# Transposing DMA transfers in place of TensorE transposes for the normalised tokens of a window-attention block

## The reference

```
f = x.transpose(0, 2, 3, 1)
f = _ln(f, g1, b1)                                   # layer norm over the 96 channels
f = jnp.roll(f, (-SS, -SS), axis=(1, 2))
win = _window_partition(f)                           # 49 tokens a window
qkv = win @ w_qkv + b_qkv
attn = jnp.einsum('bhid,bhjd->bhij', q, k) * scale   # + mask, softmax
out = jnp.einsum('bhij,bhjd->bihd', attn, v).reshape(-1, L, C)
out = out @ w_proj + b_proj                          # back to the image, rolled back
f = residual + f.transpose(0, 3, 1, 2)
m = _ln(f.transpose(0, 2, 3, 1), g2, b2)
m = jax.nn.gelu(m @ w_fc1 + b_fc1, approximate=False) @ w_fc2 + b_fc2
return f + m.transpose(0, 3, 1, 2)
```

## Time and profile before

| | |
|---|---|
| time, median of 3 runs | 2865.55 us (2864.36 to 2867.81) |
| span of the profiled execution, first to last instruction | 2865.7 us |
| PE, DVE, ACT, POOL busy | 2765.1 (96%), 2349.2 (82%), 2136.4 (75%), 1810.7 (63%) us |
| DMA engines busy, mean of 16 | 46.8% on SP's queue |

### The profile page before, as it was taken

How to read it: one execution, slowest core, us unless ns; L and a number is a source line. 1 busy time by engine, 2 the same in 40 slices (tenths; PEclk the granted TensorE clock), 3 DMA queues, 4 the chain that set the end, 5 groups by cost and what they waited for, 6 DMA issues and landing times.

```text
span 2865.7 us, 137800 instructions
## 1 busy us (share of the span) xinstructions
PE 2765.1 (96%) x55491; PEld 2312.9 (81%) x55491; DVE 2349.2 (82%) x6634; ACT 2136.4 (75%) x3464; POOL 1810.7 (63%) x2344
## 2 busy tenths in 40 slices
PE   4899999999999999999999999999999999999997
PEld 2788888888888888888888888888888888888885
DVE  7788888888888888888888888888888888888885
ACT  2677777777777777777777777777777777777774
POOL 3566666656666666666665665666666666666565
PEclk7999999999999999999999999999999999999998
DMA  2544545444554544454455455454455445454441
GB/s 72 135 125 129 132 124 132 128 130 127 131 133 125 132 131 126 129 132 124 127 132 131 125 133 133 125 132 131 126 132 132 124 129 129 129 132 128 131 117 35
DMA packets 414850, 358.86 MB, mean 125 GB/s; under 512 B 63646, under 2 KB 414176, under 8 KB 414204
## 3 DMA queue, kind: packets, MB, share of 16 engines
q1 hardware_dynamic: 414220, 350.04, 46.8%
HBM read 193.29 MB, written 154.14 MB: 121 GB/s over the span
## 4 chain that ended last, share of the span: by engine, by line
PE 91%; ACT 4%; issue 2%; DVE 2%; POOL 1%; SPq 0%; DMA 0%; POOLq 0%; DVEq 0%
PE psum L529 19%; PE psum L511 11%; PE psum L652 9%; PE psum L437 9%; PE psum L493 8%; PE psum L569 7%; PE psum L554 6%; PE psum L617 6%; PE psum L447 6%; ACT probs L713 4%; PE psum L607 3%; PE psum L455 3%; PE psum L472 2%; PE psum L596 1%; DVE nmax L849 0%
## 5 line engine op out<-in xcount | busy, mean ns | idle before, releaser
L713 ACT ACTIVATE probs<-psum 113x784 f32<-113x784 f32 x768 | 633.2, 824 | 358.9 <-PE psum L511 341.4
L849 DVE TENSOR_REDUCE nmax<-psum 113x16 f32<-113x784 f32 x768 | 745.1, 970 | 97.1 <-PE psum L493 97.0
L529 PE MATMUL psum<-vbd,probs 128*49 128x18 f32 x24576 | 642.4, 197 | 7.6 <-issue 7.0
L398 POOL TENSOR_SCALAR ve<-mv 112x7 f32<-112x7 f32 (+1 forms) x264 | 65.9, 250 | 915.0 <-PE psum L569 672.8
L529 PEld LDWEIGHTS psum<-vbd,probs 128*49 128x49 f32 x24576 | 632.2, 126 | 10.7 <-issue 10.5
L511 PE MATMUL psum<-qbd,kst 128*49 128x196 f16 x6144 | 404.7, 250 | 34.4 <-DVE xfl L884 5.7
L493 PE MATMUL psum<-kbd,qst 128*49 128x196 f16 x6144 | 404.5, 250 | 5.3 <-DVE nmax L849 3.4
L405 POOL TENSOR_TENSOR rs<-ve,half 112x7 f32<-112x7 f32 (+1 forms) x264 | 394.7, 1495 | 0.0
L410 POOL TENSOR_TENSOR xn<-xn,rs 112x672 f32<-112x672 f32 (+1 forms) x264 | 342.6, 1298 | 73.9 <-POOL rs L405 73.9
L884 DVE TENSOR_TENSOR xfl<-psum,xfh 96x784 f16<-96x784 f32 (+1 forms) x264 | 252.9, 958 | 160.7 <-ACT xfh L725 159.6
L873 DVE BATCH_NORM_STATS2 st<-tok 112x6 f32<-112x96 f32 x1824 | 318.1, 246 | 59.0 <-ACT tok L720 45.0
(11 more groups left out here) (96 smaller groups left out, 6129.4 us busy)
## 6 DMA issues: line engine op xcount, KB each, us to landing
stack_pages<-nat SPq DMA_DIRECT2D x256, 294.0 KB, 3.0
kst<-stack_pages SPq DMA_DIRECT2D x256, 220.5 KB
qbd<-stack_pages SPq DMA_DIRECT2D x1024, 55.1 KB
stack_pages<-nat SPq DMA_DIRECT2D x256, 147.0 KB, 2.0
xr<-in_x_dram SPq DMA_DIRECT2D x224, 147.0 KB, 2.7
out_dram<-yr SPq DMA_DIRECT2D x224, 147.0 KB, 2.3
qst<-stack_pages SPq DMA_DIRECT2D x256, 73.5 KB
kbd<-stack_pages SPq DMA_DIRECT2D x1024, 18.4 KB
```

The source lines that it names most:

```text
L529: last = nc.tensor.matmul(dst[:, :, h, :], probs[:, b.c % 2, h // 4, p, h % 4 * L:(h % 4 + 1) * L], vbd[:, b.c % 4, p * NH + h, :, :], sta ...
L713: nc.scalar.activation(probs[0:PR, b.c % 2, u, :, :].rearrange("j (g q) k -> j g (q k)", g=2), wide_bank()[0:PR, LEFT:LEFT + 8 * SPAN].rea ...
L849: nc.vector.tensor_reduce(dst, psum[0:PR, A:A + 2, 0:2 * CH].rearrange("i g (q h j) -> i g q h j", q=2, j=L), axis=AX.X, op=ALU.max, negat ...
```

## The change

The transposes of `back`, the ACT copy `back_high` and the DVE subtraction `back_low` are removed. POOL now makes the two float16 parts while the tokens are still on partitions (`xn16`, padded from 96 to 128 columns, with a column of ones for the biases), and SP issues two transposing transfers for each step, one for each part, that write `xfs` with channels on partitions. DVE takes over two small operations (the negated mean `less`, the variance with epsilon `ve`); POOL's two wide operations become one `tensor_scalar` for each group of 112 tokens, with two operands by partition. FC1 of both bands goes through `A`, the second after the GELU of the first, and PE's order is changed around it.

```
-            def back(t):
-                for at, g in enumerate(order + order[-1:] if odd(t) and has(t.step(HIDDEN[0])) else order):
-                    last = nc.tensor.transpose(wide_bank()[0:C, LEFT + at * SPAN:LEFT + (at + 1) * SPAN], xn[:, b.c % 2, g, :], ident[0:SPAN, 0:SPAN])
...
-                nc.scalar.activation(parts_of(xfh, b), by_channel(b), ACT.Copy).then_inc(n_high, 1)
...
-                nc.vector.tensor_tensor(parts_of(xfl, b), by_channel(b), parts_of(xfh, b), ALU.subtract).then_inc(n_low, 1)
...
+            def by_channel(b):
+                n, groups = b.c % 2, spans(b)
+                wait(sp, v_made, min(b.c - 3, NB))
+                alone(sp)
+                wait(sp, fc1_made, b.count(1, -11))
+                alone(sp)
+                for part, ready in ((HIGH, n_high), (LOW, n_low)):
+                    sp.wait_ge(ready, b.count(1, 1))
+                    alone(sp)
+                    sp.dma_start_transpose(xfs[:, b.c % 4, part, :, :].rearrange("c k t -> c (k t)")[:, 0:groups * SPAN].rearrange("c (g t) -> c g t", t=SPAN),
+                                           xn16[:, n, part, 0:groups, :].rearrange("t g c -> t (g c)")).then_inc(n_in[b.c % 4], 16)
...
             def normalise(b):
+                pool.wait_ge(stats_shared, b.count(1, 1))
+                nc.gpsimd.tensor_tensor(rs[:, n, 0:groups], ve[:, n, 0:groups], half[0:SPAN, 0:groups], ALU.pow).then_inc(root_done, 1)
+                pool.wait_ge(root_done, b.count(1, 1))
+                for g in range(groups):
+                    last = nc.gpsimd.tensor_scalar(xn[:, n, g, :], tok[:, n, g, :], less[:, n, g:g + 1], rs[:, n, g:g + 1], ALU.add, ALU.mult)
+                last.then_inc(normed, 1)
+                wait(pool, n_in[b.step(-2).c % 4], b.step(-2).used(4, N_IN))
+                nc.gpsimd.tensor_copy(xn16[:, n, HIGH, 0:groups, 0:C], xn[:, n, 0:groups, :]).then_inc(n_high, 1)
+                pool.wait_ge(n_high, b.count(1, 1))
+                nc.gpsimd.tensor_tensor(xn16[:, n, LOW, 0:groups, 0:C], xn[:, n, 0:groups, :], xn16[:, n, HIGH, 0:groups, 0:C], ALU.subtract).then_inc(n_low, 1)
...
             def expand(t, n):
                 if n == 0:
+                    for ahead in (b.step(AFTER), b.step(1 + AFTER)):
+                        pe.wait_ge(n_in[ahead.c % 4], ahead.used(4, N_IN))
+                    if has(t.step(SCORE)):
+                        pe.wait_ge(s_maxed, t.step(SCORE).count(QUADS, QUADS))
+                else:
+                    pe.wait_ge(gelu_done, t.step(HIDDEN[0]).count(1, 1))
+                most(A, w1h, w1l, b, 1)
+                rest(A, w1h, w1l, b, 1).then_inc(fc1_made, 1)
```

More of the change, by code:

```diff
@@ L126, in build @@
         st, mv = sb("st", [SPAN, 2, GROUPS, 6]), sb("mv", [SPAN, 2, GROUPS, 2])
-        ve, rs = sb("ve", [SPAN, 2, GROUPS]), sb("rs", [SPAN, 2, GROUPS])
-        xfh, xfl = sb("xfh", [FULL, 4, 2, TOK], F16), sb("xfl", [FULL, 4, 2, TOK], F16)
+        half = sb("half", [128, GROUPS])
+        ve, rs, less = (sb(name, [SPAN, 2, GROUPS]) for name in ("ve", "rs", "less"))
+        xn16 = sb("xn16", [SPAN, 2, 2, GROUPS, FULL], F16)
+        xfs = sb("xfs", [FULL, 4, 2, 2, TOK], F16)
         nat = sb("nat", [C, 4, 4, TOK], F16)
@@ L555, in turn @@
                 last.then_inc(t_made, 1)
-            def back(t):
-                b = t.step(BACK)
-                if not turns(b):
-                    return
-                pe.wait_ge(normed, b.count(1, 1))
-                if odd(t):
-                    wait(pe, gelu_done, t.step(HIDDEN[0]).count(1, 1)) if has(t.step(HIDDEN[0])) else None
-                if has(t.step(PROB)):
-                    pe.wait_ge(exp_done, t.step(PROB).count(QUADS, QUADS))
-                wait(pe, n_low, b.count(1))
-                order = list(range(spans(b)))
-                for at, g in enumerate(order + order[-1:] if odd(t) and has(t.step(HIDDEN[0])) else order):
-                    last = nc.tensor.transpose(wide_bank()[0:C, LEFT + at * SPAN:LEFT + (at + 1) * SPAN], xn[:, b.c % 2, g, :], ident[0:SPAN, 0:SPAN])
-                last.then_inc(n_made, 1)
             def queries_keys(t):
@@ L687, in step @@
                     out_transposes(t)
-                    back(t)
                     max_transpose(t)
@@ L869, in stats @@
                 n, groups = b.c % 2, spans(b)
-                wait(dve, centred, b.count(1, -1))
                 dve.wait_ge(tokens_in, b.count(1, 1))
@@ L879, in stats @@
                 last.then_inc(stats_done, 1)
-            def back_low(t):
-                b = t.step(BACK)
-                dve.wait_ge(n_high, b.count(1, 1))
-                nc.vector.tensor_tensor(parts_of(xfl, b), by_channel(b), parts_of(xfh, b), ALU.subtract).then_inc(n_low, 1)
+                dve.wait_ge(stats_done, b.count(1, 1))
+                nc.vector.tensor_scalar(less[:, n, 0:groups], mv[:, n, 0:groups, 0], -1.0, None, ALU.mult)
+                nc.vector.tensor_scalar(ve[:, n, 0:groups], mv[:, n, 0:groups, 1], EPS, None, ALU.add).then_inc(stats_shared, 1)
             def queries_keys_low(t):
@@ L923, in step @@
                 if odd(t):
-                    if turns(before.step(BACK)):
-                        back_low(before)
                     run(before, QK, queries_keys_low)
@@ L940, in step @@
                     stats(t)
-                if odd(t) and turns(t.step(BACK)):
-                    back_low(t)
                 if first(t, -TURN):
```

112 lines of the change are left out of this document (40 added, 72 removed).

## The result

| | before | changed |
|---|---|---|
| median | 2866.68 us (4 runs, 2864.36 to 2867.94) | 3115.02 us (4 runs, 3100.21 to 3123.95) |
| ratio | | 1.0859, 95% interval 1.0835 to 1.0883 |
| span of the profiled execution | 2865.7 us | 3109.9 us |

The changed kernel is 248 us slower. The forecast was 2750 us with a range up to 3080: the prediction was wrong, in the sign and in the range. The page of the changed kernel: busy time, DMA queues and the chain of work that ended last.

What follows compares the result with a forecast made beforehand. PE was taken to bound the kernel; a pair of steps would go from 21.62 to 20.67 us (21.62 - 1.60 + 0.65). Over the span 2866 - 121 + 5 for the fill gave 2750 us, range 2690 to 3080.

Steps and rivals of the forecast that it cites:

- Then SP needs 18.8 and costs nothing.: SP's queue: 14.8 us of issuing a pair plus four transposing issues at 1.0 fit in a pair of 20.67.
- Rival 1: SP's queue becomes the pace through its issue times, up to 3170 us; 25% for an issue over 1.46, 20% for slower.
- 14.8 + 4X: SP's queue: us a pair takes if that queue is the pace, present issuing plus four transposing issues.
- X: Time for SP to issue one transposing transfer: taken as 1.0 us, bounds 0.31 and 2.31.
- The base: SP's issuing a pair before the new transfers: 14.8 us, read from one even and one odd pass.
- above 1.7 the kernel is slower: SP's queue: a transposing issue over 1.46 us eats the gain, over 1.7 makes the kernel slower than before.
- The signs that I said would come first: New transfers: the prediction fails first if one issue takes over 1.5 us or lands later than 6 us after it.
- The other two on SP and PE: Signs of being wrong: SP's rows back to back with `save_high` late; PE waiting for the new transfers.
- Removing 1.60 and adding 0.65: PE's chain: transposes of `xn` removed, new waits added, so a pair goes from 21.62 to 20.67 us.
- those that I priced: PE's new waits: 0.17 us each step for maxima, 0.15 for the GELU, 0.2 around exponentials and scores; 0.69 a pair.
- the 0.30 that I took: POOL's `tensor_scalar` of 96 columns at 0.30 us each; POOL needs 18.9 of 20.67 and becomes the pace at 0.43.
- rival 2: DMA engines move transposed data slowly: a pair is 11.3 + 4Y at best, plain Y 0.77 us; 15%, nearly all slower.

Runs made afterwards that it cites:

- kernel 1: Kernel before, plus two idle transposing transfers a step on SP that write to a tile nothing reads: 3049.07 us.
- 8: Changed kernel with both parts turned by one transfer of 14 groups instead of two of 7: 2985.71 us.
- 11: Changed kernel with the row of maxima and the high parts issued by ACT instead of SP: 2827.31 us, ratio to before 0.9870.
- Kernel 14: Changed kernel with ACT issuing the row of maxima and the high parts, and one transfer turning both parts: 2809.87 us, ratio to before 0.9797.
- kernel 9: Kernel before with only FC1 of both bands through `A` and the changed order on PE and ACT: 2951.51 us.
- 16: 15 with POOL's seven small `tensor_scalar` put back to two wide operations: 2889.18 us, ratio to before 1.0072.
- kernel 2: Kernel before, plus two idle plain transfers a step on SP in pieces of 224 bytes: 2888.46 us.
- kernel 3: Kernel before, plus two idle plain transfers a step on SP in pieces of 1568 bytes: 2863.97 us.
- kernel 7: Changed kernel with SP issuing transposing and plain transfers of 1, 2, 4 and 7 groups ahead of the loop, to read issue times: 3131.41 us.
- 15: Kernel 14 with FC1 back in two pairs of banks, the old order, and rows cleared by two small matmuls: 2881.6 us, ratio to before 1.0057.
- 5: Changed kernel with each transposing transfer replaced by a plain one in pieces of 224 bytes, nothing turned: 2972.49 us.

## Why the prediction was wrong

**The step that failed is SP's queue**: "Then SP needs 18.8 and costs nothing." It needs 23.5. Rival 1, to which I gave 25%, is what happened: kernels 1, 8 and 11 show it from three sides. Both halves of 14.8 + 4X were too small.

- X, taken at 1.0 within bounds of 0.31 and 2.31, is 1.49 on average (1.43 and its half of the step between two): 6.0 us a pair instead of 4. By itself that gives 14.8 + 6.0 = 20.8, just what PE needs (20.78). So the choice of X alone would not have turned the sign.
- The base is 23.5 - 6.0 = 17.5 instead of 14.8. I read one pair and took its two quick passes as what all need. This is the row of the kernel before, behind 1404.02 in the earlier trace rows, at which the high parts are read back:

```profile
1406.06 0.31 SPq L298 DMA_DIRECT2D qst<-stack_pages  x1
```

  From storing to reading back it is 2.04 us here; from 1000 to 1600 us it was 2.45 on average in the kernel before already, and it is 2.71 now: 1.3 a pair more. I left out the steps of 0.27 ahead of the transposing issues and 0.19 behind them, 0.9 a pair. And I took off 0.50 in each pass as waiting where 0.2 stays: 0.6. That is 2.8, beside the 2.7 missing. As a mean, the queue of the kernel before took 15.4 us (21.66 less 6.2 of waiting for data), so that on balance 0.6 of the 2.7 stood in its trace; the rest came with the new transfers.
- By my rule, "above 1.7 the kernel is slower": with the true base that point is (21.66 - 17.5) / 4 = 1.04 us. The 1.0 that I took was already at it.
- The signs that I said would come first did not: the mean issue stayed under 1.5 us (single ones were longer), and no transposing transfer landed later than 5.4 us after its issue. Both look at the new transfers alone and not at the loop of the queue. The other two on SP and PE came: rows back to back with `save_high` late, and PE waiting for the new transfers.

**PE's part held in the sum, not in its terms.** Removing 1.60 and adding 0.65 was to give 20.67. Kernel 14, in whose chain SP's issues are 3%, has a median pair of 20.83 and a mean of 21.07. Its waits are not those that I priced:

```profile
PE psum L589 <- DVE nmax L848: 74.0, 236, 0.7
PE psum L503 <- DVE nmax L848: 30.5, 127, 1.1
PE psum L457 <- ACT hid L737: 3.1, 4, 0.9
```

The transpose of the maxima waits 0.31 us in each step instead of 0.17, the first scores 0.24 instead of 0.2, and the second FC1 hardly ever for the GELU, where I had 0.15: about 0.85 a pair instead of 0.69. The 0.64 of kernel 9 beside my 0.65 is partly luck: it has `back` still in it and one transpose less, and its run was expected cheaper than this sum says, which I hadn't noticed.

**POOL**: the `tensor_scalar` takes 0.41 to 0.43 us, not the 0.30 that I took, just the value at which I had POOL become the pace. It didn't, but the cover was thin: POOL is busy for 77% of the changed kernel and 85% of kernel 14, where it is 4% of the chain, and in 16 fewer operations on POOL gained nothing.

```profile
1416.19 2.86 POOL L416 TENSOR_SCALAR xn<-tok,less,rs 112x96 f32<-112x96 f32 x7 [0.21 <-POOL rs L412]
```

**The DMA engines** (rival 2) were not the pace, but a transposing transfer costs them more than the 0.77 us I took. The queue's share times the span, less that of before, over 528 transfers: kernel 1 (0.691 x 3047.3 - 0.468 x 2865.7) / 528 = 1.45 us, kernel 2 0.81, kernel 3 0.58. By rival 2's own sum 11.3 + 4 x 1.45 is 17.1 us, under PE's pace. That load shows in the landings, on which the queue stands.

The Trainium skill's price for each tile in "DMA: Bandwidth & Descriptors", section on fast descriptor generation, isn't borne out by kernel 7: one group takes 1.21 to 1.23 us and seven 1.22 to 1.29. Its "Advanced Engine Details and Errata", section on the X-bar transpose, has transposing transfers as fast as plain ones. Alone, in the first part of kernel 7, the trace agrees: seven groups take all 16 engines 1.02 us transposed (201 KB) and 0.89 us plain (176 KB), 197 and 198 GB/s. Beside the traffic of the loop it does not: a transposed piece of 256 bytes takes 20 ns alone and 30 in kernel 1, a plain one of 224 bytes 18 alone and 16 in kernel 2.

**The long issues.** A queue of its own (`q8 instruction` in the views) loads instructions in blocks of 16 KB; for which engine, the trace doesn't say. Such a block is under way during the issue of 2.62 us at 1416.46 (from 1417.04 to 1418.62); in the view of the transfers from 1416.46 to 1419.10 it is this row, which the view of the next issue, of 1.23 us, lacks:

```profile
q8 instruction: 1, 0.02, 3.8%
```

From 200 to 2600 us of the changed kernel this is so for 138 of the 139 transposing issues that took over 0.1 us more than the median, and for 82 of the 269 others in their first 1.25 us. In the part of kernel 7 ahead of the loop, where no block was loaded, none of the 24 issues was long. No run changed the loading, so that it is the cause is inferred and not shown.

What stays open: the rest of the loss of 15.

## What to carry to other kernels

Before adding transfers to a queue, add up the whole loop of that queue: every issue, the steps between them, and each landing on which it stands, as means over many periods and not from one quick pass. A transfer that is queued ahead of one on whose landing the same queue waits is paid twice: in its issue, and in the later landing (in 5 and 8, about half of what the issues saved came back as waiting). A waiting issue can be given to the engine that makes its data: here that was worth 288 us, more than the whole change had cost.

## What the runs showed of the hardware that I had not expected

- A transposing transfer takes SP about 1.24 us to issue, for 1 group as for 7, and 1.76 for 14; a plain one takes 0.52 (pieces of 1568 bytes) to 0.63 (224 bytes). The earlier trace rows has 0.31.
- Issues of every kind are now and then long (1.57 beside 0.30 for one of `kbd`). Of the 222 on SP that took over 0.5 us more than the median of their line (changed kernel, 200 to 2600 us), 213 had a block of instructions under way; of the 3046 ordinary ones, 364.
- A transposed piece of 256 bytes takes a DMA engine 20 ns alone and 30 beside the traffic of the loop, while the pieces of the other transfers take what they took before.
- A POOL `tensor_scalar` of 96 columns with two operands by partition takes 0.42 us; seven of them (2.86) take more time than two wide operations of 672 columns would at 1.31 each.
